# A decoder layer on one core: down banks by turns, the second attention's residual added in rows, and a few steps of the second pair one item later

## The reference

```
x = layernorm(x + attention(x))          # 16 heads of 16, softmax over 128 keys
x = layernorm(x + xattn(x, ctx))         # a scan over time, per feature:
    out = A + exp(u + k) * (v * B + max(t - 1, 0))        # k = x, v = ctx
    A = exp(-w) * A + inc * exp(k) * v ;  B = exp(w) * B + inc * exp(-k)
x = layernorm(x + experts(x))            # 8 experts, 256 -> 1024 -> 256, gelu
```

## Time and profile before

| | us |
|---|---|
| median of 3 runs | 947.85 (946.38 to 948.84) |
| the profiled execution, its own time | 950.24 |
| its span, first to last instruction | 948.5 |
| TensorE busy | 894.7 (94%) |
| VectorE busy | 595.9 (63%) |
| ScalarE busy | 583.7 (62%) |
| GpSimd busy | 78.1 (8%) |
| mean granted TensorE clock | 0.969 of full speed |

### The profile page before, as it was taken

One profiled execution on the slowest core, in us unless ns is written; L12 is line 12 of the kernel. 1 busy time (PEld: TensorE's weight loads), 2 busy tenths in 40 slices (PEclk: granted clock), 3 DMA queues, 4 the chain that ended last, 5 costly groups with the idle time before them and its releaser, 6 DMA issues.

```text
span 948.5 us, 17874 instructions
## 1 busy us (share of the span) xinstructions
PE 894.7 (94%) x6672; PEld 817.8 (86%) x6672; DVE 595.9 (63%) x1246; ACT 583.7 (62%) x999; POOL 78.1 (8%) x116
## 2 busy tenths in 40 slices
PE   4768879999999999999999999999999999999996
PEld 3658878789988989889988989889998999899996
DVE  5888878776756474755666564665656564423584
ACT  4548875776555766665556766655656665444683
POOL 2320012000110010200120001200110000000000
PEclk9679989999999999999999999999999999999999
DMA  7617998867755554545545555554545455655340
GB/s 224 206 50 261 342 367 284 268 223 243 239 178 169 155 172 145 178 149 184 161 142 167 179 167 164 148 178 146 177 134 178 149 173 164 193 189 167 112 134 12
DMA packets 144693, 172.43 MB, mean 182 GB/s; under 512 B 11208, under 2 KB 110816, under 8 KB 144608
## 3 DMA queue, kind: packets, MB, share of 16 engines
q1 hardware_dynamic: 144608, 171.29, 56.6%
HBM read 135.60 MB, written 35.65 MB: 181 GB/s over the span
## 4 chain that ended last, share of the span: by engine, by line
PE 86%; DVE 7%; ACT 3%; issue 2%; DMA 0%; POOL 0%; SPq 0%; POOLq 0%; DVEq 0%; ACTq 0%
PE down_ps L726 13%; PE down_ps L727 12%; PE down_ps L728 12%; PE up_ps L503 12%; PE up_ps L505 12%; PE up_ps L504 12%; PE bank L556 2%; PE bank L503 2%; PE bank L525 1%; PE bank L505 1%; PE bank L504 1%; PE bank L542 1%; DVE w_lo L884 1%; PE bank L574 1%; DVE probs L953 1%
## 5 line engine op out<-in xcount | busy, mean ns | idle before, releaser
L827 ACT ACTIVATE h_all<-up_ps,b_all 128x512 f32<-128x512 f32 (+1 forms) x296 | 182.5, 631 | 259.9 <-PE up_ps L505 258.3
L884 DVE TENSOR_TENSOR h_lo<-h_all,h_hi 128x512 fp32r<-128x512 f32 x256 | 176.8, 691 | 225.4 <-ACT h_hi L818 225.2
L726 PE MATMUL down_ps<-w_hi,h_hi 128*128 128x256 f32 x1024 | 296.6, 290 | 10.7 <-DVE acc L1066 10.7
L727 PE MATMUL down_ps<-w_lo,h_hi 128*128 128x256 f32 x1024 | 290.8, 284 | 0.0
L728 PE MATMUL down_ps<-w_hi,h_lo 128*128 128x256 f32 x1024 | 290.6, 284 | 0.0
L503 PE MATMUL up_ps<-x2t_hi,w_hi 128*128 128x512 f32 (+1 forms) x592 | 223.2, 377 | 3.8 <-ACT h_all L827 2.8
L505 PE MATMUL up_ps<-x2t_hi,w_lo 128*128 128x512 f32 (+1 forms) x592 | 217.7, 368 | 0.0
L504 PE MATMUL up_ps<-x2t_lo,w_hi 128*128 128x512 f32 (+1 forms) x592 | 217.0, 367 | 0.0
L726 PEld LDWEIGHTS down_ps<-w_hi,h_hi 128*128 128x128 f32 x1024 | 196.2, 192 | 20.0 <-issue 11.8
L727 PEld LDWEIGHTS down_ps<-w_lo,h_hi 128*128 128x128 f32 x1024 | 197.1, 193 | 6.8
L728 PEld LDWEIGHTS down_ps<-w_hi,h_lo 128*128 128x128 f32 x1024 | 196.9, 192 | 0.0
(11 more groups left out here) (195 smaller groups left out, 996.2 us busy)
## 6 DMA issues: line engine op xcount, KB each, us to landing
w_hi<-w_parts SPq DMA_DIRECT2D x200, 256.0 KB, 3.0
w_lo<-w_parts SPq DMA_DIRECT2D x200, 256.0 KB, 3.3
w_raw<-in_w_dram SPq DMA_DIRECT2D x96, 256.0 KB, 4.0
w_parts<-w_hi SPq DMA_DIRECT2D x64, 256.0 KB, 3.9
w_parts<-w_lo SPq DMA_DIRECT2D x64, 256.0 KB, 4.2
x_in<-in_x_dram SPq DMA_DIRECT2D x8, 256.0 KB, 3.9
ctx_sb<-in_ctx_dram SPq DMA_DIRECT2D x8, 256.0 KB, 3.8
out_dram<-acc SPq DMA_DIRECT2D x8, 256.0 KB, 2.5
```

What stands on the lines that cost most here:

```text
L726: nc.tensor.matmul(ps, hi, w2h[:, c, :], start=c == 0 and j == 0, stop=False, skip_group_check=True)
L727: nc.tensor.matmul(ps, hi, w2l[:, c, :], start=False, stop=False, skip_group_check=True)
L827: a = nc.scalar.activation(h_all[:, unit % HALL, k * wide:(k + 1) * wide], up_ps[unit % 2][:, k * wide:(k + 1) * wide], ACT.Gelu_apprx_tan ...
L884: return nc.vector.tensor_tensor(dst, src, hi.bitcast(F32), ALU.subtract)
```

## The change

There are three parts. A visit with one pair takes bank n mod 2 for its down products (`down_banks`), and `freed` gives the count of adds after which a bank is free since its last user, however many visits ago; with two pairs, the bank that is free earlier comes first. Visit 1 also waits for `x2_biased`. The second attention's residual y1 is no longer copied and added in the transposed form: REC_3 adds scan_a alone, and after BACK VectorE adds y1 to the bank, in place in y1, from which statistics and normalisation are then taken. And in `EARLY` of pair 1, Y1, XEXP, REC_0, REC_1, R_LOGITS and R_MAX stand one item later.

```diff
+    def down_banks(n):
+
+        return [n % 2] if len(active(n)) == 1 else [0, 1]
+
+    def freed(n, a):
+
+        users = [m for m in range(n) if down_banks(n)[a] in down_banks(m)]
+        return EVACUATED[users[-1]] + PAIR * (down_banks(users[-1]).index(down_banks(n)[a]) + 1) if users else 0
...
-        y1t = sb("y1t", [P, C, PAIR, S])
...
-        mix_a_ready = sem("mix_a_ready")
...
+        x2_sum = sem("x2_sum")
...
                 pairs = len(active(n))
+                if n == 1 and u == 0:
+                    pe.wait_ge(x2_biased, 1)
                 for k in range(2 // pairs):
                     c = u if pairs == 2 else 2 * u + k
-                    for a in range(pairs):
-                        if c == 0 and n > 0 and a < len(active(n - 1)):
-                            pe.wait_ge(added, EVACUATED[n - 1] + PAIR * (a + 1))
+                    for a in sorted(range(pairs), key=lambda a: freed(n, a)):
+                        if c == 0 and freed(n, a):
+                            pe.wait_ge(added, freed(n, a))
                         for j in range(PAIR):
                             cols = slice((k + a) * TOK + j * S, (k + a) * TOK + (j + 1) * S)
-                            ps = by_tile(down_ps[a])[:, j, :]
+                            ps = by_tile(down_ps[down_banks(n)[a]])[:, j, :]
...
                     for c in range(C):
-                        nc.scalar.activation(exp_uk[:, c], k[:, c], ACT.Exp, bias=wu[:, 1, c:c + 1])
-                    a = nc.scalar.activation(y1t[:], k, ACT.Copy)
+                        a = nc.scalar.activation(exp_uk[:, c], k[:, c], ACT.Exp, bias=wu[:, 1, c:c + 1])
                     a.then_inc(exps_ready, 1)
...
                 if s == RECUR[3]:
-                    dve.wait_ge(xa_step, 6 * p + 5)
-                    nc.vector.tensor_tensor(y1t[:], y1t[:], scan_a[:], ALU.add).then_inc(mix_a_ready, 1)
                     dve.wait_ge(xa_step, 6 * p + 6)
-                    dve.wait_ge(mix_a_ready, p + 1)
-                    nc.vector.tensor_tensor(mix, mix, y1t[:], ALU.add).then_inc(mix_ready, 1)
+                    nc.vector.tensor_tensor(mix, mix, scan_a[:], ALU.add).then_inc(mix_ready, 1)
                 if s == BACK:
                     dve.wait_ge(x2_ps, p + 1)
-                    moments_of([by_tile(bank[0])[:, j] for j in range(PAIR)], 1, ln2_step, p)
+                    nc.vector.tensor_tensor(y1[:], by_tile(bank[0]), y1[:], ALU.add).then_inc(x2_sum, 1)
+                    dve.wait_ge(x2_sum, p + 1)
+                    moments_of([y1[:, j] for j in range(PAIR)], 1, ln2_step, p)
                 if s == NORM2:
-                    norm([by_tile(bank[0])[:, j] for j in range(PAIR)], [x2_all[:, p % 2, j] for j in range(PAIR)], 1, ln2_rstd, p).then_inc(x2_ready, 1)
+                    norm([y1[:, j] for j in range(PAIR)], [x2_all[:, p % 2, j] for j in range(PAIR)], 1, ln2_rstd, p).then_inc(x2_ready, 1)
...
-                        nc.vector.scalar_tensor_tensor(out=acc[:, p % 2, t, :], in0=by_tile(down_ps[a])[:, t, :],
+                        nc.vector.scalar_tensor_tensor(out=acc[:, p % 2, t, :], in0=by_tile(down_ps[down_banks(n)[a]])[:, t, :],
...
-     WO: 22, NORM1: 24, Y1: 25, XEXP: 25, REC_0: 25, REC_1: 26, REC_2: 28, REC_3: 28, BACK: 31, NORM2: 31, R_TURN: 33,
-     R_LOGITS: 34, R_MAX: 35, R_GATE: 41, R_GATE_T: 50, R_BIAS: 51},
+     WO: 22, NORM1: 24, Y1: 26, XEXP: 26, REC_0: 26, REC_1: 27, REC_2: 28, REC_3: 28, BACK: 31, NORM2: 31, R_TURN: 33,
+     R_LOGITS: 35, R_MAX: 36, R_GATE: 41, R_GATE_T: 50, R_BIAS: 51},
```

## The result

| | us |
|---|---|
| the changed kernel, median of 9 executions | 943.94 (941.88 to 944.42) |
| the kernel before beside it, median of 9 | 947.99 (945.81 to 950.87) |
| ratio, 95% interval | 0.9947 [0.9931, 0.9964] |
| the changed kernel's profiled execution: time, span | 944.04, 942.3 |
| TensorE busy; mean granted clock | 892.0 (95%); 0.974 |

The account below looks back on a forecast made before the run. TensorE, busy 94% of the span, was taken as the bound. Gains of 0.8 (through step 4), 2.5 (visit 5) and 0.8 (end), less 0.2 (head), made 3.9 us: 943.9 us against the median 947.85, range 939.3 to 946.5.

Parts of the forecast that it names:

- step 1: Visit 1 starts in the other bank: 3.02 us wait goes, 1.9 us come before att transposes; net gain 0.2 us.
- step 4: Logits and S_0: logits' wait falls 1.71 to 0.5 us, S_0 idles 1.9 us for R_MAX; cumulative gain 0.8 us.
- step 6: The end: visit 36's 0.82 us wait goes; visit 33's wait for four adds taken at 0, bound -0.8.
- step 3: Residual added in rows: 0.2 us lost in the head, nothing on pair 2, whose chain had 0.8 us of room.
- Step 2: Visit 3 and moved steps: 1.53 us wait goes, about 4 us idle ends before QK; gain so far 1.6 us.
- The Trainium skill's rule that was weighed: SBUF interfaces shared with VectorE: x_bo would hold the head's norm, sum 0.4 us less; without it, 0.2 more.
- the clock falls again, -1.6: Behind TensorE's 1.9 us idle ahead of S_0 of pair 2, low clock takes 1.6 us off the gain.
- Step 5: Visit 5: six matmuls run under the 2.02 us wait, 1.3 us remains, low stretch goes; gain taken 2.5 us.
- (a): Rival: clock kept at the stalls of steps 1 and 4, GpSimd holds nothing; 8.5 us gained, 939.3 us; chance 0.2.
- (b): Rival: the weight traffic by DMA becomes the bound; 946 us; chance 0.1.
- (c): Rival: first stall unlocks nothing, another order of the queue paces TensorE through visits 1 to 4; 944.8 us; chance 0.15.
- (d): Rival, slower: row-wise sum grows BACK's chain past R_TURN's room on pairs 2 to 7; 951.1 us; chance 0.04.

Follow-up runs that it names:

- xlow_early: The changed kernel with X_LOW (xt_lo) of pair 2 one item earlier in EARLY: 939.43 us, ratio 0.9906 to the kernel before.
- moves_only: The kernel before with only Y1, XEXP, REC_0, REC_1, R_LOGITS and R_MAX of pair 1 one item later: 944.12 us, ratio 0.9949 to the kernel before.
- residual_only: The kernel before with only the residual added in rows: 949.41 us, ratio 0.9998 to the kernel before.
- split_late: The changed kernel with GpSimd's splits of v of pair 2 held until R_MAX has read the logits: 941.96 us, ratio 0.9927 to the kernel before.

## Why the prediction came out right, and where it did not

**The number.** 943.9 forecast, 943.94 measured. That it agrees to 0.1 us is luck. The sum was made for the profiled execution, and there 3.9 us were forecast and 6.2 measured. Of the difference, 1.4 us is a low stretch of the head (step 1), which the change did not cause, and 1.6 the low stretch behind S_0's wait that did not come (step 4); visit 33 takes 0.35 back (step 6) and the head 0.3 (step 3). The other half of the luck is the base: the medians of the kernel before went from 947.99 to 949.59, and 947.85 is at their low end. Against the 949.22 of the 41 executions the change gives 5.3 us.

**Step 1** holds. No wait for bank 1; 1.81 us ahead of the att transposes (forecast 1.9), low clock behind. They start 3.3 us earlier, of which 1.9 was forecast. The rest, 1.4, is the low stretch at 77.8 that after does not have. It is no effect of the banks: visit 0 is the same in both. In all five traces with the wait of 2 us at 78 the low clock of the head had ended by 69; where it lasted to 72 or later the wait was 0.85 at most, and the up unit started at the same time (77.85 before, 77.77 after) without low clock behind it.

**Step 2** holds in what it forecast: QK starts at 132.29 (forecast 133.6, and 1.4 came with the head) after 3.88 us of idle (forecast 4), low clock behind; Y1's 1.53 is gone. xlow_early shows that VectorE's queue set this wait. One reading in it was wrong: it puts REC_1 ahead of the add of visit 2, and in VectorE's order of after the add (128.70) stands ahead of REC_1 (its first instruction at 129.49). For QK that is the same, for xt_lo stands behind both. With one bank it is not: in moves_only D(3,0) waits 2.75 us for that add instead of 3.48.

**Step 3**: the head was taken at 0.2 us lost, with 0.5 as the bound. From the normalisation of y of pair 0 to the up unit by 78 us it is 29.1 us in before and 29.7 in after, so 0.5 to 0.6 are lost there; in the time of residual_only that cannot be seen. The mechanism was half right. The normalisation of x in after over the run (ns min/median/max), then pair 3's in VectorE's timeline of after, and x_bo beside it on GpSimd:

```profile
L911 DVE TENSOR_SCALAR x<-y,moments,rstd x16: 407/812/834, 60.8 to 785.1; 128x256 f32<-128x256 f32 x16
```

```profile
350.25 1.57 DVE L911 TENSOR_SCALAR x<-y,moments,rstd 128x256 f32<-128x256 f32 x2 [0.58 <-POOL rstd L1166]
```

```profile
350.18 1.49 POOL L1175 TENSOR_TENSOR x_bo<-x_in,bo_all 128x256 f32<-128x256 f32 x2
```

The same two in the kernel before:

```profile
355.08 0.99 DVE L902 TENSOR_SCALAR x<-bank,moments,rstd 128x256 f32<-128x256 f32 x2
```

```profile
354.57 1.88 POOL L1167 TENSOR_TENSOR x_bo<-x_in,bo_all 128x256 f32<-128x256 f32 x2
```

I had put 407 ns in place of 540 on every pair. The median is 812: from SBUF the normalisation is held by x_bo, from PSUM it was not (0.99 beside the same add). So on the five pairs where x_bo is beside it (0 and 3 to 6) the change costs VectorE some 0.5 to 0.6 us a pair instead of saving 0.26; on pairs 1, 2 and 7 it is 407 to 414 ns as forecast. No R_TURN from 205 us on waits for it. The Trainium skill's rule that was weighed (GPSIMD Engine Reference, Specifications) was the one to follow for the hold: 1.54 with x_bo, 0.73 without. The sum took neither choice but a value between them; the trace gives the one with the hold.

**Step 4**: 0.46 ahead of the logits (forecast 0.5), 2.07 ahead of S_0 (1.9), w_lo and h_lo held by GpSimd, and split_late shows that hold. The term that failed is "the clock falls again, -1.6": the 3.4 us behind S_0's wait ran at 1.00, in both traces of the change, and of five such waits in all kernels one had low clock behind it. From 1.71 and 2.02 us with low clock and 1.53 without I had made a rule of length alone; between 1.7 and 2.1 us the length does not settle it.

**Step 5** holds: six matmuls under the wait, 1.22 left (forecast 1.3), full clock after. **Step 6** holds for visit 36; visit 33's four adds, taken at nothing with a bound of 0.8, cost 0.35.

**What the sum left out** is that the parts are not additive. The steps gave the banks steps 1, 5 and 6, and the moves parts of 2 and 4. Measured, banks alone and moves alone give each the whole. The rest of the change on top of the banks trades 1.53 for 1.2 more ahead of QK, and 1.71 for 0.46 and 2.07: 0.5 us more idle. The forecast had those terms with the right signs; what it lacked was the same sum for the banks without the moves.

**The rivals.** (a), clock kept and nothing held: the clock was kept behind S_0's wait, but not in step 1, and GpSimd did hold. (b), the traffic: a DMA did release a w_hi once, a sign that the prediction had named for being wrong. ScalarE waited 1.52 us (0.20 before) for the w_lo copy at 83.72. But TensorE has no wait of 0.25 us or more from 78 to 102 us, and past its start none of its waits ends on a DMA: false. (c), the first stall unlocks nothing: false, as step 1 shows. (d), BACK's chain: 0.47 forecast, 1.3 with the hold (0.73 and 0.58), below the 1.5 from which it would decide, and no wait stands ahead of R_TURN from 205 us on; false. The Trainium skill's rule on transposes (TensorE: Matmul & The Clock Gate) would make the transposes' places the likelier to lose clock. By the table 5 of 9 waits ahead of transposes did and 13 of 19 of the others, and the transposes themselves follow the clock: four of att took 0.66 us at 1.00 and 1.04 at 0.50 (the two lines above). The traces do not agree with the rule.

## What to carry to other kernels

A wait of the engine that bounds the kernel costs its length and, if it is long enough, nearly as much again in clock: a low stretch of 3.4 us stood behind every wait of 2.6 us and more and behind no wait up to 1.54, so two waits of 1.2 us should be cheaper than one of 2.4. So ask of an edit not only how much idle time it removes but what lengths it leaves. In between, at 1.7 to 2.1 us, give the low stretch a chance (18 of 28 here) and not a certainty. An equal gain of two parts is not yet an equal mechanism either: part of what moves_only won was a wait that kept its length and fell at a better moment. Ask of each part what it gives without the others, for the next late value may be the same queue's: here VectorE's order (xt_lo one item earlier, 4.5 us) was worth about as much as a second bank. And where executions of one kernel lie 6 us apart, the trace shows only one of them: compare its mean clock with those of the timed runs before its time is used as a base.

## What the runs showed of the hardware

The same kernel ran at a mean granted clock of 0.966 to 0.975, and its time went with it, 951.5 to 945.5 us. The Trainium skill, TensorE: Matmul & The Clock Gate (Part 1), calls the count of slow matmuls variable from run to run. The 41 executions agree, and so does the head of the two pairs of traces (a first low stretch of 13.7 or 17.1 us); from 75 us on each pair shows the same low stretches.

Behind waits of 1.80 to 1.84 us at one place TensorE's clock fell in four traces and stayed in three, and a shift of the wait by some 0.5 us went with the difference.

A normalisation of 128x256 with one SBUF operand took 0.4 us alone and 0.8 beside GpSimd's add; with a PSUM operand it took 0.5 beside the same add (1.57 and 0.99 for two). The Trainium skill, VectorE: DVE Perf Modes (Why PSUM operands drop a tier), says that PSUM gives VectorE one read port and the faster form needs two of SBUF. The trace agrees that it is slower alone (540 against 407 ns); that it then has nothing to share with GpSimd is my reading of the two rows.
